# Gated cross-attention block with one quantised product and routed experts: gate values kept in h's PSUM bank, the first tile of x in halves, quarter stores at the end, and another order of all calls

## What is computed

```python
def fake_quant(x, scale, zp):
    q = jnp.clip(jnp.round(x / s + z), 0.0, 255.0)
    return (q - z) * s
...
x = x + tanh(g_xattn[0]) * matmul(fake_quant(layernorm(x), ...), fake_quant(ctx, ...))
...
y = layernorm(x)
logits = einsum('bsd,ed->bse', y, route_w)
topk_v, topk_idx = top_k(logits, 1)
route_weight = one_hot(topk_idx[..., 0], 8) * topk_v
h = einsum('bsd,erd->bser', y, A)
out = einsum('bser,eor->bso', route_weight[..., None] * h, Bw)
x = x + tanh(g_ffn[0]) * out
```

## Time and profile before

| what | value |
|---|---|
| median of 3 runs | 389.33 us (389.13 to 390.45) |
| the profiled execution's own time | 389.91 us |
| its span | 388.1 us |
| PE busy | 338.8 us (87%) |
| DVE busy | 292.3 us (75%) |
| ACT busy | 186.1 us (48%) |
| POOL busy | 166.4 us (43%) |
| DMA, all large queues | 87.11 MB, 76.4% of 16 engines |

### The profile page before, as it was taken

One profiled execution on the slowest core, in us unless ns is written; L12 is line 12 of the kernel. 1 busy time (PEld: TensorE's weight loads), 2 busy tenths in 40 slices (PEclk: granted clock), 3 DMA queues, 4 the chain that ended last, 5 costly groups with the idle time before them and its releaser, 6 DMA issues.

```text
span 388.1 us, 5794 instructions
## 1 busy us (share of the span) xinstructions
PE 338.8 (87%) x2204; PEld 186.8 (48%) x2230; DVE 292.3 (75%) x578; ACT 186.1 (48%) x119; POOL 166.4 (43%) x219
## 2 busy tenths in 40 slices
PE   0169899999999879998596999999999899998883
PEld 0145344657667536435162364645464546464461
DVE  3989975787988888875688576798764566758785
ACT  1697574868668414488289442422640602440020
POOL 2766566232113740389449226183635162524000
PEclk9999999999999999999699899999999999999999
DMA  7999999096557995999989943976849961277625
GB/s 304 407 366 386 395 387 353 22 389 207 177 194 277 185 233 199 353 246 320 190 131 331 252 150 69 315 160 192 213 85 249 230 118 20 54 119 169 258 110 216
DMA packets 93618, 87.63 MB, mean 226 GB/s; under 512 B 71812, under 2 KB 72836, under 8 KB 89476
## 3 DMA queue, kind: packets, MB, share of 16 engines
q1 hardware_dynamic: 93568, 87.11, 76.4%
q10 hardware_dynamic: 12, 0.00, 0.0%
HBM read 52.49 MB, written 16.78 MB: 178 GB/s over the span
## 4 chain that ended last, share of the span: by engine, by line
PE 64%; DVE 19%; DMA 10%; issue 3%; ACT 2%; POOL 1%; ACTq 0%; DVEq 0%
PE main L1407 44%; DMA qa<-q 6%; PE hp L1428 3%; PE hp L1432 3%; PE hp L1429 3%; PE outp L1470 3%; PE outp L1472 2%; PE outp L1471 2%; DVE whs L1007 2%; DVE pick L993 2%; DVE bn L839 2%; DMA xs<-in_x 2%; DVE xs L1015 1%; DMA prow<-in_g_ffn 1%; DVE wh L996 1%
## 5 line engine op out<-in xcount | busy, mean ns | idle before, releaser
L1407 PE MATMUL main<-q,qa 128*128 128x512 bf16 x875 | 204.7, 387 | 6.8 <-DMA qa<-q 2.4
L1407 PEld LDWEIGHTS main<-q,qa 128*128 128x128 bf16 x896 | 87.8, 99 | 110.2 <-issue 7.2
L533 POOL TENSOR_TENSOR yn<-y,yn 128x2048 f16<-128x2048 f32 x12 | 48.9, 4075 | 32.9 <-ACT y L694 32.7
L967 DVE SCALAR_TENSOR_TENSOR xs<-main,cc,xs 128x512 f32<-128x512 f32 x52 | 38.6, 743 | 29.8 <-PE main L1407 29.6
L540 POOL CAST q<-c 128x2048 bf16<-128x2048 int8 x24 | 45.2, 1905 | 24.9 <-ACT c L650 17.1
L650 ACT ACTIVATE c<-stage,zpc,inv 128x2048 int8<-128x2048 f32 x24 | 49.6, 2086 | 11.2 <-DMA stage<-in_ctx 11.1
L518 POOL TENSOR_SCALAR ve<-mv 128x1 f32<-128x1 f32 x16 | 3.5, 220 | 90.8 <-DVE mv L974 90.8
L1015 DVE SCALAR_TENSOR_TENSOR xs<-outp,tsc,xs 128x512 f32<-128x512 f32 x52 | 36.8, 734 | 6.0 <-PE outp L1472 5.8
L688 ACT ACTIVATE yn<-xs,sc 128x2048 f16<-128x2048 f32 x10 | 20.9, 2092 | 42.5 <-POOL sc L527 42.5
L662 ACT ACTIVATE x<-xs,sc 128x2048 int8<-128x2048 f32 x13 | 27.2, 2090 | 27.6 <-POOL sc L513 25.1
L839 DVE BATCH_NORM_STATS2 bn<-xs 128x6 f32<-128x512 f32 x52 | 32.0, 676 | 7.8 <-DMA xs<-in_x 7.8
(11 more groups left out here) (122 smaller groups left out, 423.6 us busy)
## 6 DMA issues: line engine op xcount, KB each, us to landing
stage<-in_ctx SPq DMA_DIRECT2D x24, 1024.0 KB, 7.6
xs<-in_x SPq DMA_DIRECT2D x13, 1024.0 KB, 6.7
out<-xs SPq DMA_DIRECT2D x12, 1024.0 KB, 5.7
yT<-in_ctx SPq DMA_DIRECT2D x4, 1024.0 KB, 10.6
y<-in_ctx SPq DMA_DIRECT2D x4, 1024.0 KB, 10.6
c<-in_x SPq DMA_DIRECT2D x3, 1024.0 KB, 7.1
out<-c SPq DMA_DIRECT2D x3, 1024.0 KB, 6.3
c<-in_L_ffn_A SPq DMA_DIRECT2D x1, 1024.0 KB, 15.9
```

The costliest lines, as they stand in the source:

```text
L533: pool.tensor_tensor(yn[:, 1, :], y[:, :], yn[:, 0, :], ALU.subtract).then_inc(s_ylo_made, 1)
L967: dve.scalar_tensor_tensor(out=xcol(t, c0, c1), in0=mainp[n % 2][:, :], scalar=cc[:, :], in1=xcol(t, c0, c1), op0=ALU.mult, op1=ALU.add).t ...
L1407: last = pe.matmul(mainp[n % 2][:, :], q1T(t)[:, k, :], q2[:, nb, k, :], start=(k == 0), stop=(k == KC - 1))
```

## The change

Five things are changed.

1. In the gate, `hl` and `wh` move from SBUF into free columns of the PSUM bank `hp`. The mask `pick` goes: one instruction compares and multiplies in a single step, and the largest logit is multiplied into `tsc` instead. `h_group` and `h_rows_high` now wait until the previous gate has written `whs` (`s_wh_ready`), and no longer only until `hl` is written.
2. Tile 0 of `x` is quantised by ScalarE in two halves, the second half of the columns first, and widened by VectorE in two halves. `turn_q1` and `take_q1T` are now called per half, and the product's run 0 and run 2 wait for one half each.
3. The last tile is stored in four pieces of 512 columns in place of two of 1024.
4. The product now waits for its pieces in all four ramp tiles, where it waited in tile 0 only. `norm_high` also waits for the previous `low_rows`.
5. The calls of all five lists are in a new order. `column_sums`, `unit_terms` and the like do nothing with these inputs.

VectorE's scaling of A and of the router weights, the last step of `scale_a` and `scale_router`, is now a call of its own (`mult_a`, `mult_router`) that stands a few calls later.

The lists `OUT_ACT`, `LAST_ACT`, `LOW_DVE` are empty and `N4` is 0, so `scale_part`, `add_part`, ScalarE's `norm_group`, VectorE's `low_rows`, and the `mult_a` and `mult_router` of GpSimd and ScalarE, all of which the diff adds, are not called; `bank_of(n)` still gives `mainp[n % 2]`.

```diff
-        hl = sb("hl", [P, WC], f32)
-        pick = sb("pick", [P, ER], f32)
-        wh = sb("wh", [P, ER], f32)
+        hl, wh = hp[:, 144:144 + WC], hp[:, 288:288 + ER]
...
             def gate(t):
-                dve.tensor_tensor(hl[:, :], hp[:, 0:WC], wscale[:, :], ALU.mult).then_inc(s_h_read, 1)
+                dve.tensor_tensor(hl, hp[:, 0:WC], wscale[:, :], ALU.mult).then_inc(s_hl_done, 1)
...
-                dve.tensor_scalar(pick[:, :], eid[:, :], idxf[:, :], top8[:, 0:1], ALU.is_equal, ALU.mult)\
-                   .then_inc(s_pick_done, 1)
-                dve.wait_ge(s_pick_done, n)
-                dve.tensor_tensor(wh[:, :], hl[:, 0:ER], pick[:, :], ALU.mult).then_inc(s_wh_done, 1)
+                dve.scalar_tensor_tensor(out=wh, in0=eid[:, :], scalar=idxf[:, :], in1=hl[:, 0:ER],
+                                         op0=ALU.is_equal, op1=ALU.mult).then_inc(s_wh_done, 1)
...
-                dve.tensor_scalar(tsc[:, t:t + 1], am[:, 1:2], th[:, 1:2], None, ALU.mult).then_inc(s_tsc_done, 1)
+                dve.tensor_scalar(tsc[:, t:t + 1], am[:, 1:2], th[:, 1:2], top8[:, 0:1], ALU.mult, ALU.mult)\
+                   .then_inc(s_tsc_done, 1)
...
             def h_rows_high(t):
-                pe.wait_ge(s_h_read, t)
+                pe.wait_ge(s_wh_ready, t)
...
+            def affine_first(half):
+                c0, c1 = half * D // 2, (half + 1) * D // 2
+                act.wait_ge(s_norm1, 1)
+                act.activation(x8[:, c0:c1], xcol(0, c0, c1), ACT.Identity, bias=sc1[:, 0, 2:3], scale=sc1[:, 0, 1:2])\
+                   .then_inc(s_affine1 if half else s_affine_half, 1)
...
+            def widen_first(half):
+                c0, c1 = half * D // 2, (half + 1) * D // 2
+                dve.wait_ge(s_affine1 if half else s_affine_half, 1)
+                dve.tensor_copy(q1[:, c0:c1], x8[:, c0:c1]).then_inc(s_q1_ready if half else s_q1_half, 1)
...
-            widen_x(0)
+            widen_first(0)
+            widen_first(1)
             stats1(2)
+            stats1(3)
+            take_q1T(0, 0)
             see_q1(0)
             widen_x(1)
-            take_q1T(0)
-            stats1(3)
+            take_q1T(0, 1)
...
-            turn_q1(0)
-            turn_q1(1)
-            turn_q1(2)
+            turn_q1(0, 0)
+            turn_q1(0, 1)
+            turn_q1(1, 0)
+            turn_q1(1, 1)
             column_sums(0, [0])
             main(0, 0, 0)
             main(0, 0, 1)
-            turn_q1(3)
             main(0, 0, 2)
+            turn_q1(2, 0)
+            turn_q1(2, 1)
...
             load_x(0)
             load_x(1)
-            load_ctx(0)
             load_x(2)
             load_x(3)
+            load_ctx(0)
...
-            load_ctx(28)
+            load_ctx(29)
+            flip_high(6)
             store(4)
-            load_ctx(29)
-            load_x(9)
-            flip_high(6)
+            load_ctx(30)
             flip_low(6)
             flip_q1(8)
-            load_ctx(30)
+            load_x(9)
+            flip_high(7)
...
             main(8, 0, 0)
+            main(8, 1, 0)
             main(8, 0, 1)
+            main(8, 1, 1)
             main(8, 0, 2)
             main(8, 0, 3)
-            main(8, 1, 0)
-            main(8, 1, 1)
             main(8, 1, 2)
...
+            for g in range(NB):
+                sp.wait_ge(s_outp_read, NB * (len(OUT_DVE) - 1) + g + 1)
+                sp.dma_start(out_t[T - 1][:, g * NW:(g + 1) * NW], xcol(T - 1, g * NW, (g + 1) * NW))\
+                  .then_inc(s_quarter_stored, 16)
```

More of the change, by code:

```diff
@@ L31 @@
 UNIT = {u: i for i, u in enumerate(RAMP + [(t, nb) for t in range(G, T) for nb in range(NB)])}
-QD = 6
-YD = 3
-YP = {0: 0, 1: 1, 2: 2, T - 1: YD}
+QT = [0, 1, 2, 3, 4, 5]
+YT = [0, 1, 2, 15]
+QN = [t for t in range(T) if t not in QT]
+YN = [t for t in range(T) if t not in YT]
+LOW_DVE = []
+OUT_ACT = []
+LAST_ACT = []
+OUT_DVE = [t for t in range(T) if t not in OUT_ACT]
+N4 = 0
 TURNS = [("q", 0), ("q", 1), ("q", 2), ("q", 3), ("a", 0), ("b", 0), ("q", 4), ("y", 0), ("y", 1), ("y", 2), ("q",
@@ L393, in _ @@
             load_ctx(11)
+            load_x(4)
             load_ctx(12)
@@ L441, in _ @@
             load_x(11)
+            load_x(12)
             flip_high(8)
@@ L445, in _ @@
             store(6)
-            load_x(12)
+            flip_high(9)
             load_x(13)
-            flip_high(9)
             flip_low(9)
@@ L455, in _ @@
             flip_q1(12)
+            store(8)
+            load_x(15)
             flip_high(11)
-            store(8)
             flip_low(11)
-            load_x(15)
             flip_q1(13)
-            store(9)
             flip_high(12)
@@ L469, in _ @@
             flip_low(14)
+            store(9)
             store(10)
@@ L1329, in wait_turn, with turn_q1 @@
                     pe.wait_ge(s, count)
-            def turn_q1(t):
-                pe.wait_ge(s_q1_ready, t + 1)
-                for half in range(2):
-                    wait_turn("q", t, half)
-                    for k in range(KC // 2):
-                        c = half * KC // 2 + k
-                        last = pe.transpose(turnb[half][:, k * P:(k + 1) * P], q1[:, c * P:(c + 1) * P], idb[:, :])
-                    last.then_inc(s_q1T_turned, 1)
+            def turn_q1(t, half):
+                if t == 0 and half == 0:
+                    pe.wait_ge(s_q1_half, 1)
+                elif t == 0 or half == 0:
+                    pe.wait_ge(s_q1_ready, t + 1)
+                wait_turn("q", t, half)
+                for k in range(KC // 2):
+                    c = half * KC // 2 + k
+                    last = pe.transpose(turnb[half][:, k * P:(k + 1) * P], q1[:, c * P:(c + 1) * P], idb[:, :])
+                last.then_inc(s_q1T_turned, 1)
             def turn_a(c):
@@ L1412, in turn_y @@
             def turn_y(t, g):
[L1413 removed]
+                if t < T - 1:
                     if g == 0:
[L1415 removed]
+                        pe.wait_ge(s_y_ready, YT.index(t) + 1)
                 else:
[L1417 removed]
+                    if g in LAST_ACT:
+                        pe.wait_ge(s_y_late, LAST_ACT.index(g) + 1)
+                    else:
+                        pe.wait_ge(s_y_ready, YT.index(t) + g + 1 - len([a for a in LAST_ACT if a < g]))
                 if g < 2:
@@ L1569, in _ @@
             main(3, 3, 1)
+            turn_y(0, 0)
+            turn_y(0, 1)
+            main(3, 3, 2)
+            main(3, 3, 3)
             turn_y(0, 2)
             turn_y(0, 3)
-            main(3, 3, 2)
+            column_sums(4, range(NB))
+            main(4, 0, 0)
+            main(4, 1, 0)
             h_group(0, 0)
@@ L1575, in _ @@
             h_group(0, 2)
+            turn_y(1, 0)
             h_group(0, 3)
-            turn_y(1, 0)
-            main(3, 3, 3)
             turn_y(1, 1)
-            column_sums(4, range(NB))
-            main(4, 0, 0)
             main(4, 0, 1)
@@ L1717, in _ @@
             main(8, 3, 2)
+            h_rows_low(7)
+            main(8, 2, 2)
+            main(8, 2, 3)
             main(8, 3, 3)
@@ L1811, in _ @@
             main(12, 3, 2)
+            main(12, 2, 1)
+            main(12, 2, 2)
+            main(12, 2, 3)
             main(12, 3, 3)
+            expert_product(9, 2)
             expert_product(9, 3)
```

697 lines of the change are left out of this document (382 added, 315 removed).

## The result

The changed kernel takes 373.4 us (median of 4 executions, 371.2 to 376.4) against 389.9 beside it on the same chip. The ratio is 0.958, with a 95% interval of 0.951 to 0.965. The forecast was 374 us, with a range of 368.5 to 382. The profiled execution took 373.27 us, its span is 371.5 us, where that of before was 388.1.

What follows compares the result with a forecast made beforehand. The prediction took TensorE, busy 87% of the span, to set the pace. Its terms, 17.0 + 0.9 - 2.5 + 0 = 15.4 us, off the profiled 389.91 us and adjusted to the median, gave 374 us, range 368.5 to 382.

Steps and rivals of the forecast that it cites:

- Gate, 17.0 us: VectorE's gate: PSUM operands end holding by GpSimd, removing 12.66 us of TensorE waits and 4.3 us of half clock.
- A gate is 0.3 us shorter: VectorE's gate: dropping `pick` (0.35 us) makes each gate 0.3 us shorter, no extra for PSUM; only gate(15) is bare.
- Start, 0.9 us: Ramp: unit (0,1) waits until 41.4 us, not 42.82; less one turning of A, 0.9 us gained.
- New waits, 2.5 us lost: SyncE's new order: late `flip_q1(7)`, `flip_q1(9)` and pieces 29 and 31 cost 5 us, 2.4 already there; 2.5 lost.
- `hp` closed longer, nothing: PSUM bank `hp` stays shut until `whs` is written, 2.4 us after the scaling; the next h comes later, cost nothing.
- Tail, nothing: After the last statistics: last addition 0.4 us later, smaller last store saves 0.3 to 0.4 us; sum nothing.
- the waits come back as transfers: Rival, chance 0.23: busy DMA engines make transposes or pieces late at gates 5 and 6; 379 to 386 us.
- All of it comes through: Rival, chance 0.15: the whole gate and start gain arrives and the DMA waits vanish too; 369 us.
- The gates are still held: Rival, chance 0.06: GpSimd also holds gate instructions mixing PSUM and SBUF, so the 17.0 us stay; 387 to 391 us.
- Units in pairs: Rival, chance 0.06: interleaved units in about 18 places make TensorE wait for VectorE's additions, 1.4 us per pair; 396 us.

Runs made afterwards that it cites:

- the gate alone: The kernel before with only the gate exchanged for the one in PSUM, old order kept: 377.2 us, ratio 0.968.
- the order-alone kernel: The changed kernel with the old gate in SBUF, so only the order, start and tail are new: 390.6 us, ratio 1.004.
- the kernel in sequence: The changed kernel with TensorE's units of tiles 4 to 15 one after the other, four runs each in sequence: 373.7 us, ratio 0.959.
- the kernel with the step in all lists: Kernel before with PSUM gate, SyncE's load_x(9) behind three transposes, tile 9's steps moved back on VectorE, GpSimd, ScalarE: 377.9 us, ratio 0.969.

## Why the prediction was right, point by point

The sum was 15.4 us and 16.6 came (spans). The main term and its mechanism were right. That the sum came so close is in part luck: the start and the middle gave 1.2 and 1.4 us more than forecast, the tail took 1.3 us. The terms:

- *Gate, 17.0 us.* Right in mechanism, and about right in size: waits and half clock are gone, and the gate alone shows 12.4 us by the medians (14.2 by the spans) plus the 5.0 that its next wait and the clock behind it cost.
- *A gate is 0.3 us shorter.* Mis-sized: gate(0), not held in either, takes 2.90 us against 3.09. `pick` is gone (0.35), but the fused instruction takes 0.36 for 0.29, the scale with `top8` in it 0.25 for 0.19, and `whs` from PSUM 0.34 for 0.29. The kernel with `wh` in SBUF isolates the last: 0.28 there, so some 0.06 us is the price of PSUM. The reduction takes 0.29 from either. The rule weighed in the prediction (the Trainium skill, "Perfetto Trace Analysis", Optimizing Scalar/DVE Operations) has that 0.06 us for every instruction; the trace shows it in one. That one is a `tensor_scalar`, the only one of these forms for which the passage on the ports above names a fast mode; whether losing that mode is the price was not tested.
- *Start, 0.9 us.* Under-sized. The product from 24.36 us and the second turning at 22.68 are as forecast, but unit (0,1) runs at 39.91, not 41.4: the scaling of A was priced at the 2.4 us of before, which were themselves held; it takes 1.28. On the way the product stands 1.84 us at 28.90 and 0.48 us at 43.58 for a piece. The first addition after the scales of A, B and the router are worked out ends at 81.81 us against 83.94, so 2.1 us are gained in all. That is not the same in every profile: of the seven profiles with the new start, the order-alone kernel's among them, five end this addition at 81.3 to 81.8 us and two (half stores, old tail) at 83.6. TensorE's clock is full from 26.0 us on here and from 30.7 before, but what that gives is not shown: with `wh` in SBUF it is full only from 28.5 and the addition ends at 81.7 all the same. The halves of tile 0, in which the prediction saw a first turning 0.6 us sooner, brought 0.2 us there (14.88 us against 15.06) and nothing in the time.
- *New waits, 2.5 us lost.* Over-sized. Beside `flip_q1(7)` four short waits of 0.4 to 0.7 us remain. The waits for transfers are 3.1 us in all against 2.4, so 0.7 us are lost between 45 us and the tail. `flip_q1(9)` costs 0.66 us, the pieces 29 and 31, counted at 1 to 2 us each, nothing.
- *`hp` closed longer, nothing.* Right: no wait for the bank appears. (It stays closed 2.6 us after the scaling, in gate(0) from 98.56 to 101.15 us, and not 2.4.)
- *Tail, nothing.* Mis-sized. From the last statistics to the end of the span it is 22.2 us against 20.9: 1.3 us lost. The last addition comes 18.1 us after the last statistics, with 17.8 forecast and 17.3 before. The last quarter lands 3.6 us after its issue, where the last half took 3.0: the small store, from which the prediction expected 0.3 to 0.4 us, lands later, with the other quarters in flight ahead of it.

In the three stretches of the table: 2.1 us gained at the start (forecast 0.9), 15.9 in the middle (forecast 17.0 - 2.5 = 14.5), 1.3 lost in the tail (forecast 0). Together 16.7, where the rounded spans give 16.6. The signs that the prediction named appeared: no gate instruction above 0.36 us, no wait over 1.56 us between 45 us and the tail, transfers as the largest cause of what waits remain.

Of the rivals, *the waits come back as transfers* has its mechanism, but only without the order: it is what the gate alone shows. In the changed kernel the DMA share from 174 to 189 us is still 1.05, have 1.10, and TensorE is busy 14.79 of the 15 us. A full queue did not hurt here, with the right transfer in front. *All of it comes through* did not happen either: 3.1 us of waits for transfers remain. *The gates are still held* is refuted by the rows above. *Units in pairs* is refuted by 0.7 us of waits for VectorE's additions and by the kernel in sequence.

## What to carry to other kernels

Look for instructions whose maximum is many times their median: they are held, and a changed operand (one in PSUM) frees them at the price of 0.06 us or nothing. An order made for quick gates loses with slow ones (390.6 us) and the reverse leaves 3.7 us behind, so change the instruction and the order together, and move a load only with its consumers and with what stands behind these in each list. In a tail without cover, two more additions behind the gate cost more than an earlier gate gave (18.1 us against 17.15 to the last addition).

## What the runs showed of the hardware

- The issue of a transpose on SyncE ends about when the last transfer ahead of it in the queue has landed: in the changed kernel at 178.15 us with a landing at 177.55 (2.84 us long, one transfer of 1 MB in flight) and at 188.26 with one at 188.48 (6.12 us, two), in the kernel with the step in all lists at 207.41 with one at 207.74 (12.68 us, four). Until then nothing behind it in SyncE's list is issued.
- A wait of 2.3 to 2.4 us on TensorE was followed by half clock in four profiles of six, at the same place of nearly the same program; in a seventh, with 2.55 us, it was not. The last addition comes 1.3 to 1.4 us later for it, but the last store then lands 0.5 to 1.1 us sooner after its issue.
- The `tensor_scalar` of 2048 columns on A (SBUF to SBUF) took 2.35 us where a cast of GpSimd had begun before it (32.37 us, it began at 32.99), and 1.28 us where it began first (37.43 us, the cast at 37.55). In the second case the cast took 2.91 us for its usual 1.9. So what a trace shows as an instruction's price can itself be held time, and which of the two is held depended on which came first.
